# Two tiles of P made at the head of the edge block, relative rows loaded ahead of Q's last store, 16-bit tables

## What is computed

```
xn   = layernorm(x)
feat = [xn[dst], xn[src] - xn[dst]]
msg  = relu(feat @ W1 + b1) @ W2 + b2
x    = x + segment_sum(msg, dst) / (deg + 1e-8)
x    = x + experts(layernorm(x))          # top 2 of 8, gelu, weighted sum
```

## Time and profile before

| | |
|---|---|
| median of three runs | 1121.46 us |
| profiled execution, first to last instruction | 902.9 us |
| first block | 0 to 65.3 us |
| edge block | 65.3 to about 593 us |
| PE busy | 834.7 us (92%) |
| DVE busy | 651.0 us (72%) |
| ACT busy | 628.3 us (70%) |
| POOL busy | 602.4 us (67%) |

### The profile page before, as it was taken

How to read it: one execution, slowest core, us unless ns; L and a number is a source line. 1 busy time by engine, 2 the same in 40 slices (tenths; PEclk the granted TensorE clock), 3 DMA queues, 4 the chain that set the end, 5 groups by cost and what they waited for, 6 DMA issues and landing times. The chain is left out here.

```text
span 902.9 us, 17755 instructions
## 1 busy us (share of the span) xinstructions
PE 834.7 (92%) x4088; PEld 652.2 (72%) x4089; DVE 651.0 (72%) x1764; ACT 628.3 (70%) x1393; POOL 602.4 (67%) x615
## 2 busy tenths in 40 slices
PE   6997999999999989989999999989999999999997
PEld 3444767767676666766666666768888999999996
DVE  6846888888888888878888887756894455455443
ACT  4425788888888888888898889845554555555553
POOL 2317777777777777777777777659404677776764
PEclk9998999999999999999999999999999999999999
DMA  8547777878888778888887878819852344444443
GB/s 255 171 150 220 247 239 245 247 234 251 240 243 236 247 231 243 241 238 238 245 248 235 230 233 264 228 49 281 265 139 54 59 73 75 81 71 68 76 71 45
DMA packets 91000, 169.47 MB, mean 188 GB/s; under 512 B 17604, under 2 KB 56910, under 8 KB 90840
## 3 DMA queue, kind: packets, MB, share of 16 engines
q0 software_dynamic: 43696, 122.35, 49.8%
q1 hardware_dynamic: 46232, 44.79, 17.0%
q10 hardware_dynamic: 944, 0.92, 0.4%
HBM read 146.98 MB, written 21.43 MB: 187 GB/s over the span
## 5 line engine op out<-in xcount | busy, mean ns | idle before, releaser
L1001 POOL DMA_INDIRECT gath<-q_rows,idx_t x408 | 391.9, 960 | 138.8 <-issue 93.3
L1068 DVE SCALAR_TENSOR_TENSOR h_lo<-bank,h_hi 128x512 fp32r<-128x512 f32 x327 | 219.4, 682 | 40.1 <-ACT h_hi L1250 38.0
L1250 ACT ACTIVATE h_hi<-bank 128x512 fp32r<-128x512 f32 x327 | 191.0, 598 | 45.5 <-DVE bank L1063 20.9
L1231 ACT ACTIVATE bank<-gath 128x512 f32<-128x512 f32 x287 | 173.4, 604 | 14.3 <-DMA gath<-q_rows,idx_t 10.5
L1384 PE MATMUL bank<-p_hi,ohT 128*128 x287 | 123.4, 430 | 42.8 <-ACT bank L1231 40.3
L1428 PE MATMUL agg_ps<-h_hi,oh 128*128 128x512 f32 x408 | 161.9, 397 | 0.3 <-DVE h_lo L1068 0.2
L1429 PE MATMUL agg_ps<-h_lo,oh 128*128 128x512 f32 x408 | 161.3, 395 | 0.0
L1995 POOL DMA_INDIRECT out<-y_out,sca_i x56 | 93.7, 1673 | 49.0 <-issue 15.9
L1384 PEld LDWEIGHTS bank<-p_hi,ohT 128*128 128x128 f32 x287 | 54.1, 189 | 91.2 <-issue 83.0
L1385 PE MATMUL bank<-p_lo,ohT 128*128 x287 | 113.9, 397 | 0.0
L2099 PE MATMUL bank<-tokT,fw_now 128*128 128x128 f32 x896 | 109.3, 275 | 0.8 <-ACT tokT L2055 0.8
(11 more groups left out here) (287 smaller groups left out, 1276.6 us busy)
## 6 DMA issues: line engine op xcount, KB each, us to landing
rows_sb<-rel_blocks SPq DMA_DIRECT2D x102, 128.0 KB, 4.3
fw<-in_L_ffn_W SPq DMA_DIRECT2D x16, 512.0 KB, 5.1
gath<-q_rows,idx_t POOLq DMA_INDIRECT x408, 4.4
q_rows<-q_buf SPq DMA_DIRECT2D x25, 256.0 KB, 2.4
out<-x_all SPq DMA_DIRECT2D x28, 128.0 KB, 3.8
x_all<-in_x SPq DMA_DIRECT2D x25, 128.0 KB, 2.7
xm_rows<-xt SPq DMA_DIRECT2D x25, 128.0 KB, 3.0
x_all<-in_x SPq DMA_DIRECT2D x2, 640.0 KB, 10.3
```

Of the source, the lines that this page charges most:

```text
L1001: pool.indirect_dma_start(out=gath[:, j % RING, :], out_offset=None, in_=q_rows[:, :], in_offset=bass.IndirectOffsetOnAxis(ap=idx_t[:, j:j ...
L1068: dve.scalar_tensor_tensor(out=h_lo[:, j % LO_RING, :], in0=z_of(slot0, j), scalar=0.0, in1=h_hi[:, j % HI_RING, :].bitcast(F32), op0=ALU. ...
L1231: actv.activation(z_of(slot0, j), gath[:, j % RING, :], ACT.Copy).then_inc(s_seed, 1)
L1250: actv.activation(h_hi[:, j % HI_RING, :], z_of(slot0, j), ACT.Relu).then_inc(s_hi, 1)
```

## The change

PE no longer makes P of the tiles 0 and 1 at the end of the first block. It makes them at the head of the edge block, after `s_bc` and ahead of all clearing, into the same two banks and with the same semaphore. SP loads the first three groups of relative rows after the 24th store of Q (t == NT - 2) and ahead of the wait for the 25th. The tables `tile_of_slot`, `tile_row`, `tile4_i`, `group_tile` and `turn_i` hold unsigned 16-bit integers in place of 32-bit ones.

```diff
+U16 = mybir.dt.uint16
-    tile_of_slot = nc.dram_tensor("tile_of_slot", (SC, P), I32, kind="Internal").ap()
+    tile_of_slot = nc.dram_tensor("tile_of_slot", (SC, P), U16, kind="Internal").ap()
...
-        tile_row = sb("tile_row", [1, SC * P], I32, edge_ctx)
+        tile_row = sb("tile_row", [1, SC * P], U16, edge_ctx)
...
-        tile4_i = sb("tile4_i", [SC, P], I32, b_ctx)
+        tile4_i = sb("tile4_i", [SC, P], U16, b_ctx)
...
-        group_tile = sb("group_tile", [NG, GROUP], I32, b_ctx)
+        group_tile = sb("group_tile", [NG, GROUP], U16, b_ctx)
...
-        turn_i = sb("turn_i", [P, 2, MS], I32)
+        turn_i = sb("turn_i", [P, 2, MS], U16)
...
                     if t == 4:
                         sp.dma_start(w1g[:, 0:KD, :], ...)
-                sp.wait_ge(s_relst, 16)
-                for q in range(REL_RING):
-                    load_rel(sp, q)
+                    if t == NT - 2:
+                        sp.wait_ge(s_relst, 16)
+                        for q in range(REL_RING):
+                            load_rel(sp, q)
...
-                def first_p(t):
-                    pe.wait_ge(s_q, NT - 3 + t + 1)
-                    for k in range(KD):
-                        ins = pe.matmul(bank[t][:], x_all[:, t, k * P:(k + 1) * P], w1d[:, k, 0:H], start=(k == 0), stop=(k == KD - 1))
-                    ins.then_inc(s_p_ps, 1)
...
-                pe.wait_ge(s_wdiff, 1)
-                for t in range(READY):
-                    first_p(t)
...
                 pe.wait_ge(s_bc, 6)
+                pe.wait_ge(s_wdiff, 1)
+                for t in range(READY):
+                    for k in range(KD):
+                        ins = pe.matmul(z_bank[t], x_all[:, t, k * P:(k + 1) * P], w1d[:, k, 0:H], start=(k == 0), stop=(k == KD - 1))
+                    ins.then_inc(s_p_ps, 1)
```

## The result

The changed kernel took 1110.6 us (median of four runs, 1108.8 to 1115.7) beside 1122.4 us for the kernel before: a ratio of 0.9878, 95% interval 0.9839 to 0.9917. Forecast was 1122.0 with no change.

What follows compares the result with a forecast made beforehand. POOL's gather pace was taken to bound the edge block, so only the first gather's start counted: 902.9 + 0.5 = 903.4 us span, with 218.6 us around it 1122.0 us against 1121.46; range 1117.5 to 1126.5 us.

Steps and rivals of the forecast that it cites:

- The fixed time of 218.6 us: Time taken to lie around the 902.9 us span, added to the forecast span of 903.4 us.
- the bound: Edge block: POOL (GpSimd) issues 408 gathers at 1.26 us each without being held; the engines behind keep pace.
- such waits: Edge block: POOL waits over 0.3 us would prove the forecast wrong, as the engines behind it would then count.
- The 16-bit tables: Register loads on PE and ACT: size read is little of the time, so narrower entries cost 0.
- The rival with slower loads: PE's load in each group slower with 16-bit entries; at twice the time +53 us, 1174 us; chance 0.05.
- The head: First block's end to the edge block's start: block ends 2.2 us earlier, first gather +0.5 us, PE/ACT/DVE chain 0.
- the block's end: End of the first block, with SP last: moves from 65.3 to 63.1 us, 2.2 us earlier.
- The first gather: POOL's start in the edge block: 66.8 us against 66.33, +0.5 us; within 0.8 us of before, chance 0.60.
- The stall for gain_T: DVE's wait at the head of the edge block, until 78.56 us before: shrinks to about 76.4, costed at nothing.
- The first seed: ACT's start of seeding in the edge block: 70.6 us in both kernels, cost 0.
- The condition that the prediction named for it: PE's clock at 1.2 GHz in the moved P products after its longer pause: +3.6 us, covered by the ring.
- its rival with a free store: Q's 25th store isn't held by the loads: first gather 0.6 to 1.4 us earlier, 1120.1 to 1120.9 us; chance 0.22.

Runs made afterwards that it cites:

- e1: Kernel before with its 32-bit tables, plus register masks ahead of the waits that use a table's value: 905.9 us, ratio 1.0026.
- e6: Changed kernel with both moves, but 32-bit tile tables with masks in the waits, only turn_i at 16 bits: 1112.2 us, ratio 1.0043 to the kernel before.
- e13: Kernel before with 16-bit tables alone, neither move: 1097.1 us, ratio 0.9913 to the kernel before.
- e3: Kernel before with the five tables at 16 bits and nothing else: 958.3 us, ratio 1.0601 to the kernel before.
- e10: Kernel before with 16-bit tables alone, run again: 958.5 us, ratio 1.0629 to the kernel before.
- e15: Both moves with 32-bit tables and masks, TensorE loading 8 tile numbers every 8 slots, not 4 every 4: 1110.8 us, ratio 1.0028 to the kernel before.
- e4: Changed kernel with the relative rows loaded behind Q's last store again: 956.8 us, ratio 1.0571 to the kernel before.
- e2: Changed kernel with both moves, but its five tables at 32 bits and masks in the waits: 906.2 us, ratio 1.0021 to the kernel before.
- e11: Changed kernel with masks on the tile numbers in the waits of ScalarE and TensorE: 958.5 us, ratio 1.0617 to the kernel before.
- e5: Changed kernel itself, run again beside the kernel before: 1095.9 us, ratio 0.9889.
- e8: Changed kernel, ScalarE loading 1 value every 16 slots and 4 every fourth slot, not 17 at once: 1108.1 us, ratio 1.0000 to the kernel before.
- e9: Changed kernel itself, run beside a kernel before of about 904 us: 958.4 us, ratio 1.0626.

## Why the prediction was wrong

**The fixed time of 218.6 us is the first step that failed.** It set a span of 902.9 beside a median of 1121.46 and called the difference time around the program. The two are one program at two levels: e1 takes 905.9 us with a span of 903.6, e6 takes 1112 with 1110.2. All that was read of the pace, distances and waits was level A, and the times to forecast were level B. A difference of 24% between a span and its runs had to be a question and not a term. With it failed what the prediction said of the bound, that GpSimd is never held: in the profile after it stands 50 times for over 2 us in the edge block. The prediction had named such waits as a sign of being wrong.

**The 16-bit tables were costed at 0, and that was the mis-sized term.** The fixed time falls out of a comparison of the two kernels, this term doesn't: it measured -11 us at level B (e13) and +54 at level A (e3, e10), and the change as a whole measured -12. The argument went from 4 values in 1.00 us and 17 in 1.26 to "the size of what is read is little of the time". It laid TensorE's load beside ScalarE's, and both were of 32 bits. For narrower entries that inference doesn't hold: 17 values of 16 bits took 3.60 us, and 8 (turn_i) 1.87 against 0.57. The rival with slower loads had the mechanism and nearly the size (+53 us; +54 were measured at level A), but on the wrong engine: TensorE's four values kept their 0.99 us, and ScalarE, whose load it didn't price, became the one that others wait for. That +53 and +54 agree is luck.

The Trainium skill, page "Runtime: NRT & Kernel Launch", section "Instruction fetch mechanics", gives a TENSOR_LOAD as about 200 ns a register even in bulk; it speaks of loads from HBM, and these read SBUF. The 16-bit loads agree (3.60 / 17 = 0.21 us, 1.87 / 8 = 0.23), TensorE's four 32-bit values too (0.25). ScalarE's seventeen 32-bit values and GpSimd's eight don't, with 0.07 each, and for these the measurement decides. In e15 TensorE loads eight at once:

```profile
L944 PEldq TENSOR_LOAD <-tile_row x52: 512/958/1970, 71.8 to 791.7; - x52
```

That is 0.12 us a value, in about the time of four. So with 32 bits neither the count nor the bytes alone give the price. A reading that fits these four rows, and that no run tests, is that four 32-bit values that begin at a multiple of four in the table come in one step of 0.2 to 0.3 us and others one by one: TensorE's loads begin six slots ahead, ScalarE's at a multiple of 16.

**The head went nearly as worked out.** Loads at 61.03 for 61.0, last store at 62.49 for 62.5, the block's end at 63.3 for 63.1. The first gather was at 66.69 for 66.8, but that agreement says little: it lies at 65.70 to 66.72 in the 13 traces with both moves and at 65.84 to 66.65 in the six with neither, so +0.5 us is inside the scatter. In e4, with P moved and the loads behind the store, it is at 65.19. That is one trace, and it fits what was expected of e4: the loads ahead of the store use up what the move of P wins. The stall for gain_T shrank by 4 us (2.2 foreseen). The first seed was at 70.30 in e2 and 72.30 in the profile after, for 70.6. The condition that the prediction named for it came true in part: TensorE's products took 5.37 us at a granted clock of 0.59 (64 to 68 us) in the profile after, and 3.67 at 1.00 in e2. The slow form stands in five of the 14 traces with P moved, at both levels, and it doesn't show in the total: at level A e4, which has it, takes 956.8 us, and e11, which hasn't, 958.5. Two bounds of the prediction are off by a little and change nothing: its rival with a free store gives 64.6 + 0.7 = 65.3, so 1.0 to 1.4 us and not 0.6 to 1.4, and 256 KB at two loads' distance take 0.94 us and not 0.8 to 0.9. **That GpSimd's pace swallows what the head wins** is shown at level A by e2 against e1: 0.0% of difference.

**At level B the gain is the tables' doing.** e13 has the gain without the moves, e6 the moves without the gain. None of the rivals had this case. What is shown: at level B the engines stand still while gathers are under way, and mostly start when their packets have ended. In e5 and e13 ScalarE's 3.6 us load begins within 0.3 us of the end of a pause of GpSimd in 23 of 26 cases, as the 1.26 us load of e6 does in 22, and 16 slots take 27.2 us in place of 28.1 (27.9 in the profile after, taken beside the slower kernel before of the first comparison). Why a longer stop of ScalarE just there brings 0.9 us is not settled; that splitting it loses the gain (e8) is all that the runs say. What starts the pauses, and why only at level B, is open too.

## What to carry to other kernels

Compare a profile's span with the timed runs before anything else; where they differ by more than a few microseconds, the profile may show another regime than the one that is timed (here 1.8 to 2.3 us lie around a span, in every execution of the record, and 218.6 lay between), and a forecast needs a case for each. Price a register load by engine, count and width of its values from a row of the same width, or bound it from above by the dearest rate per value that the trace has (1.00 / 4 = 0.25 us here, which gives 4.3 us for seventeen and would have put ScalarE among the rivals). A value loaded but not used may not be loaded at all: count the instructions of an experiment before reading its time.

## What the runs showed of the hardware

- A bulk register load on ScalarE of 17 values: 1.26 us out of a 32-bit table (e1), 3.60 out of a 16-bit one (e9); of 8 values on GpSimd 0.58 and 1.87. On TensorE four values take 1.00 and 0.99, eight 32-bit ones 0.96 (e15).
- At level B the engines behind the gathers stop for about 3 us every 8 slots, and the first time for far longer (VectorE 14.8 us in e6), while the DMA engines go on at 195 to 212 GB/s; short instructions of TensorE's queue can take 0.70 us in place of 0.04. In e6 the stop ends 0.7 us behind the last packet (median).
- The same program, on the same chip position, takes 903 us in one comparison and 1108 in another, with every run of a comparison at one level.
